# Attention on one Trainium2 core: the split maxima turned on their own and added by a product of three rows, the queries turned once

## What is computed

```python
q = (h @ w_q).reshape(b, l, N_HEADS, HEAD_DIM)        # 16 heads of 16
k = (h @ w_k).reshape(b, l, N_KV_HEADS, HEAD_DIM)     # 4 key heads
logits = jnp.einsum('bhqd,bkhd->bhqk', q, k) * scale
logits = jnp.where(causal[None, None], logits, -jnp.inf)
attn = jax.nn.softmax(logits, axis=-1)
ao = jnp.einsum('bhqk,bkhd->bqhd', attn, v).reshape(b, l, d)
```

## Time and profile before

| | |
|---|---|
| time, median of 3 runs | 2175.52 us (2172.95 to 2183.99) |
| the profiled execution | 2186.68 us, span 2185.4 us |
| busy: PE, PEld | 1665.2 us (76%), 1176.6 us (54%) |
| busy: DVE, ACT, POOL | 1023.0, 845.0, 457.5 us |

### The profile page before, as it was taken

One profiled execution on the slowest core, in us unless ns is written; L12 is line 12 of the kernel. 1 busy time (PEld: TensorE's weight loads), 2 busy tenths in 40 slices (PEclk: granted clock), 3 DMA queues, 4 the chain that ended last, 5 costly groups with the idle time before them and its releaser, 6 DMA issues. The chain is left out here.

```text
span 2185.4 us, 40696 instructions
## 1 busy us (share of the span) xinstructions
PE 1665.2 (76%) x16744; PEld 1176.6 (54%) x16744; DVE 1023.0 (47%) x1865; ACT 845.0 (39%) x1646; POOL 457.5 (21%) x511
## 2 busy tenths in 40 slices
PE   3678888888888888879888888783495577756958
PEld 2346665665666756657656666572253334433535
DVE  2435646556456566465565564633514543231131
ACT  2234444444444454444444444342221234411122
POOL 1111312322313222223132222231003201031100
PEclk9778999999989999899999899996698676767979
DMA  2101102111002011111110110101000000002010
GB/s 56 22 20 25 31 24 42 23 22 33 22 14 50 23 24 28 26 23 41 23 33 12 33 28 17 23 11 58 0 0 16 0 1 1 1 0 58 0 49 19
DMA packets 179800, 50.95 MB, mean 23 GB/s; under 512 B 151616, under 2 KB 174784, under 8 KB 179616
## 3 DMA queue, kind: packets, MB, share of 16 engines
q1 hardware_dynamic: 168240, 47.15, 9.7%
q10 hardware_dynamic: 11376, 1.19, 0.5%
HBM read 34.48 MB, written 13.83 MB: 22 GB/s over the span
## 5 line engine op out<-in xcount | busy, mean ns | idle before, releaser
L987 POOL TENSOR_TENSOR og<-og,sz 128x256 f32<-128x256 f32 x128 | 93.0, 726 | 753.4 <-DVE og L934 531.6
L435 PE MATMUL banks<-wv,xT 128*128 128x512 f32 x256 | 143.1, 711 | 74.3 <-DVE Yv L795 46.4
L795 DVE SCALAR_TENSOR_TENSOR Yv<-banks,cwall,Yv 128x1022 f32<-128x1022 f32 (+2 forms) x96 | 122.4, 1275 | 84.2 <-ACT Yv L651 83.6
L435 PE MATMUL banks<-wqk,xT 128*128 128x512 f32 x256 | 126.8, 641 | 23.8 <-DVE Yk L795 23.8
L435 PEld LDWEIGHTS banks<-wv,xT 128*128 128x128 f32 x256 | 55.3, 227 | 148.0 <-issue 148.0
L573 PE MATMUL banks<-wz,xT 128*128 128x256 f32 x512 | 132.0, 405 | 0.0
L638 PE MATMUL banks<-wo,oT 128*128 128x256 f32 x512 | 126.5, 391 | 0.8 <-ACT oT L788 0.8
L772 ACT ACTIVATE V<-banks,skd 128x128 f32<-128x128 f32 x192 | 59.9, 363 | 153.3 <-PE banks L602 153.0
L573 PEld LDWEIGHTS banks<-wz,xT 128*128 128x128 f32 x512 | 105.7, 209 | 23.1 <-issue 6.7
L638 PEld LDWEIGHTS banks<-wo,oT 128*128 128x128 f32 x512 | 95.6, 194 | 14.5 <-ACT oT L788 2.4
L617 PE MATMUL banks<-V,A 128*128 128x128 f32 x512 | 90.4, 305 | 11.9 <-ACT V L774 11.9
(11 more groups left out here) (332 smaller groups left out, 3758.0 us busy)
## 6 DMA issues: line engine op xcount, KB each, us to landing
cm_d<-CM SPq DMA_DIRECT2D x32, 256.0 KB, 4.2
wqk<-in_L_attn_W_qkvz SPq DMA_DIRECT2D x8, 512.0 KB, 4.5
wv<-in_L_attn_W_qkvz SPq DMA_DIRECT2D x8, 512.0 KB, 3.7
wz<-in_L_attn_W_qkvz SPq DMA_DIRECT2D x16, 256.0 KB, 2.8
wo<-in_L_attn_W_out SPq DMA_DIRECT2D x16, 256.0 KB, 3.0
blk<-cm_d SPq DMA_DIRECT2D x128, 16.0 KB, 1.8
t_d<-tb SPq DMA_DIRECT2D x16, 128.0 KB, 1.7
u_d<-ub SPq DMA_DIRECT2D x16, 128.0 KB, 1.8
```

Of the source, the lines that this page charges most:

```text
L435: ins = pe.matmul(bank[b][:, :], xT[:, d, b * S + of_batch, :], w[:, d, :], start=(d == 0), stop=(d == KD - 1))
L795: v.scalar_tensor_tensor(y, pair[0][:, :, 0:T - j], conv_w(k, t)[:, 3 - j:4 - j], y, ALU.mult, ALU.add).then_inc(s["tap"].sem, 1)
L987: pool.tensor_tensor(og[:, n, :, :], og[:, n, :, :], sz[q % 2][:, b, :].rearrange("p (h d) -> p h d", h=VR), ALU.mult).then_inc(s["osz"].s ...
```

## The change

The negated, split maxima no longer go into `qs`. They get a tile of their own, `n3`, with 32 columns for each `g` of which three are used. `pe_turn_max` turns it with 8 transposes for all four heads, and one ScalarE copy brings it to `nT`, where head `g` has rows 32`g` to 32`g`+2. The second turning of the queries, 32 transposes and four copies, is gone. In the scores by key the first product takes 96 rows in place of 128, and a new product of three rows, `one` by `nT`, of the same width, adds the maxima of each head. `n3` and `one` are filled once by GpSimd, ahead of its first copy of queries.

```diff
@@ -1400,26 +1400,37 @@
 
 
 def attention(nc, c, pair, bank, am, m, t_):
-    s = signals(nc, {"qs": 1, "qTt": 8, "qTe": 8, "sc": 16, "mx": 16, "nm": 6, "e": 16, "ex": 16, "pv": 8, "oTe": 2, "oTt": 2, "rec": 2, "on": 2})
+    s = signals(nc, {"qs": 1, "qTt": 4, "qTe": 4, "fill": 2, "nTt": 1, "nTe": 1, "sc": 16, "mx": 16, "nm": 6, "e": 16, "ex": 16, "pv": 8, "oTe": 2, "oTt": 2, "rec": 2, "on": 2})
     qb, qs, kT, vp, by_query, by_key = (t_[n] for n in ("qb", "qs", "kT", "vp", "by_query", "by_key"))
     qT = am("qT", [P, KVH, TT, P], BF16)
     mx, nm = am("mx", [P, TT, KVH]), am("nm", [P, TT, KVH])
+    n3, nT, one = am("n3", [P, TT, KVH, SLOT], BF16), am("nT", [P, TT, P], BF16), am("one_b", [P, P], BF16)
     pt, oT = am("ptile", [P, 2, KVH, T]), am("l1_oT", [P, T])
     rec, ao = am("rec", [P, QT, KVH]), am("ao", [P, TT, REP, KVH, HD])
     t_["ao"] = ao
 
     def on_gpsimd(pool):
+        pool.memset(n3[:, :, :, :], 0.0).then_inc(s["fill"].sem, 1)
+        pool.memset(one[:, :], 1.0).then_inc(s["fill"].sem, 1)
         for j in range(REP):
             if j:
-                pool.wait_ge(*s["qTt"](7, j - 1))
+                pool.wait_ge(*s["qTt"](3, j - 1))
             for i, part in enumerate(Q_PARTS):
                 ins = pool.tensor_copy(qs[:, :, :, i * HD:(i + 1) * HD], qb[:, part, :, j * KVH * HD:(j + 1) * KVH * HD].rearrange("p t (g e) -> p t g e", g=KVH))
             ins.then_inc(s["qs"].sem, 1)
 
-    def pe_turn_q(pe, j, go):
+    def pe_turn_max(pe, j):
+        pe.wait_ge(*s["qTe"](2, j))
+        for t in range(TT):
+            ins = pe.transpose(bank[4].bitcast(BF16)[:, t * P:(t + 1) * P], n3[:, t, :, :].rearrange("p g i -> p (g i)"), c["identb"][:, :])
+        ins.then_inc(s["nTt"].sem, 1)
+
+    def pe_turn_q(pe, j):
+        if j:
+            pe.wait_ge(*s["nTe"](0, j - 1))
         for g in range(KVH):
-            if g >= 2 or go:
-                pe.wait_ge(*s["qTe"](4 * go + g - 2, j))
+            if g >= 2:
+                pe.wait_ge(*s["qTe"](g - 2, j))
             for t in range(TT):
                 ins = pe.transpose(bank[4 + g % 2].bitcast(BF16)[:, t * P:(t + 1) * P], qs[:, t, g, :], c["identb"][:, :])
             ins.then_inc(s["qTt"].sem, 1)
@@ -1438,7 +1449,7 @@
         if b:
             pe.wait_ge(*s["on"](0, j))
         else:
-            pe.wait_ge(*s["qTe"](7, j))
+            pe.wait_ge(*s["qTe"](3, j))
         for u in range(QT):
             ins = pe.transpose(bank[5][:, u * P:(u + 1) * P], oT[:, u * P:(u + 1) * P], c["ident"][:, :])
         ins.then_inc(s["oTt"].sem, 1)
@@ -1448,7 +1459,7 @@
             if j:
                 pe.wait_ge(*s["on"](1, j - 1))
             pe.wait_ge(*s["qs"](0, j))
-            pe_turn_q(pe, j, 0)
+            pe_turn_q(pe, j)
             for t in range(TT):
                 b, q = divmod(t, QT)
                 width = (q + 1) * P
@@ -1464,18 +1475,21 @@
                         ins = pe.matmul(pair[gp][:, h, width - P:width], c["identb"][:, :], by_query[:, :], start=False, stop=True, skip_group_check=True)
                     ins.then_inc(s["sc"].sem, 1)
             pe.wait_ge(*s["nm"](5, j))
-            pe_turn_q(pe, j, 1)
+            pe_turn_max(pe, j)
             for b in range(B):
                 for kt in range(QT):
                     t = b * QT + kt
                     width = T - kt * P
                     for gp in range(2):
                         if t == 0:
-                            pe.wait_ge(*s["qTe"](4 + 2 * gp + 1, j))
+                            pe.wait_ge(*s["nTe"](0, j))
+                            pe.wait_ge(*s["fill"](1))
                         if t:
                             pe.wait_ge(*s["ex"](2 * (t - 1) + gp, j))
                         for h in range(2):
-                            pe.matmul(pair[gp][:, h, 0:width], kT[:, 2 * gp + h, t, :], qT[:, 2 * gp + h, t:(b + 1) * QT, :], start=True, stop=False, skip_group_check=True)
+                            pe.matmul(pair[gp][:, h, 0:width], kT[0:USED, 2 * gp + h, t, :], qT[0:USED, 2 * gp + h, t:(b + 1) * QT, :], start=True, stop=False, skip_group_check=True)
+                            rows = slice((2 * gp + h) * SLOT, (2 * gp + h) * SLOT + 3)
+                            pe.matmul(pair[gp][:, h, 0:width], one[rows, :], nT[rows, t:(b + 1) * QT, :], start=False, stop=False, skip_group_check=True)
                             ins = pe.matmul(pair[gp][:, h, 0:P], c["identb"][:, :], by_key[:, :], start=False, stop=True, skip_group_check=True)
                         ins.then_inc(s["e"].sem, 1)
                     if kt == 0 and j:
@@ -1495,14 +1509,13 @@
 
     def on_scalar(act):
         for j in range(REP):
-            for go in range(2):
-                for g in range(KVH):
-                    act.wait_ge(*s["qTt"](4 * go + g, j))
-                    if go:
-                        act.wait_ge(*s["sc"](15, j))
-                    elif j:
-                        act.wait_ge(*s["e"](15, j - 1))
-                    act.copy(qT[:, g, :, :], bank[4 + g % 2].bitcast(BF16).rearrange("p (t i) -> p t i", t=TT)).then_inc(s["qTe"].sem, 1)
+            for g in range(KVH):
+                act.wait_ge(*s["qTt"](g, j))
+                if j:
+                    act.wait_ge(*s["e"](15, j - 1))
+                act.copy(qT[:, g, :, :], bank[4 + g % 2].bitcast(BF16).rearrange("p (t i) -> p t i", t=TT)).then_inc(s["qTe"].sem, 1)
+            act.wait_ge(*s["nTt"](0, j))
+            act.copy(nT[:, :, :], bank[4].bitcast(BF16).rearrange("p (t i) -> p t i", t=TT)).then_inc(s["nTe"].sem, 1)
             for t in range(TT):
                 b, kt = divmod(t, QT)
                 width = T - kt * P
@@ -1525,12 +1538,15 @@
             v.wait_ge(*s["mx"](15, j))
             v.tensor_scalar(nm[:, :, :], mx[:, :, :], -1.0, None, ALU.mult).then_inc(s["nm"].sem, 1)
             v.wait_ge(*s["nm"](0, j))
-            v.wait_ge(*s["qTt"](3, j))
+            if j:
+                v.wait_ge(*s["nTt"](0, j - 1))
+            else:
+                v.wait_ge(*s["fill"](0))
             for i in range(3):
-                v.tensor_copy(qs[:, :, :, USED + i], nm[:, :, :]).then_inc(s["nm"].sem, 1)
+                v.tensor_copy(n3[:, :, :, i], nm[:, :, :]).then_inc(s["nm"].sem, 1)
                 v.wait_ge(*s["nm"](1 + 2 * i, j))
                 if i < 2:
-                    v.tensor_tensor(nm[:, :, :], nm[:, :, :], qs[:, :, :, USED + i], ALU.subtract).then_inc(s["nm"].sem, 1)
+                    v.tensor_tensor(nm[:, :, :], nm[:, :, :], n3[:, :, :, i], ALU.subtract).then_inc(s["nm"].sem, 1)
                     v.wait_ge(*s["nm"](2 + 2 * i, j))
             for b in range(B):
                 v.wait_ge(*s["oTt"](b, j))
```

## The result

The changed kernel takes 2267.38 us (median of 4 runs, 2264.86 to 2273.05), before it is 2174.25 us in the same measurement. The ratio is 1.0422, 95% interval 1.0385 to 1.0459: slower by 4.2%, where I had forecast 2.0% and a range that ended at 2244 us. The direction was right, and the size forecast was less than half of the one measured. The profiled executions have spans of 2185.4 and 2271.8 us, 86.4 apart.

The account below looks back on a forecast made before the run. TensorE was taken to bound the scores by key: 13.85 us added a round, less 1.24 of pauses and 1.79 for turning, gave +10.8, +43.3 in four; with +0.2 once, 2175.5 + 43.5 = 2219.0 us, range 2190 to 2244.

Parts of the forecast that it names:

- TensorE bounds the scores by key and gets all of the added work: In the scores by key, added TensorE work first fills 1.24 us of pauses, then lengthens the round.
- The turning, 1.79 us a round: Ahead of the scores by key: 8 transposes and one copy let the first product begin after 2.09 us, before 3.88.
- Once in the stage: GpSimd's fills of `n3` and `one` add 1.1 us, hiding the exponentials' table load saves about 0.9: together +0.2.
- The passage, 0.10 us: Scores by key: switching between whole-array and few-row products costs 0.10 us each way, 64 times a round, 6.4 us.
- The clock: In the scores by key, few-row products keep TensorE at 0.50 through tiles 0, 1 and the first values, then 1.00.
- the first values raise the clock: In the scores by key and values, the first values, with 128 rows and four heads side by side, bring 1.00.
- the pauses of 1.24: TensorE's waits in the scores by key that added work fills: 0.60, 0.24 and 0.40 us a round.
- 0.50 throughout: Rival: TensorE's clock stays at 0.50, columns of tiles 2 to 7 cost double, some 10 us a round more: 2259; chance 0.05.
- The early rise: Rival: the clock rises in tile 0 of the scores by key as before, 2.33 us a round less: 2209.7; chance 0.20.
- Cheap passages: Rival: switching to few-row products and back costs 0.05 us each way, 3.2 us a round less: 2206; chance 0.12.

Follow-up runs that it names:

- The kernel without the product: Against the changed kernel, the product adding the maxima is left out and the scores by key take 128 rows again: 2167.34 us, ratio 0.9948.
- The kernel with half the passages: Changed kernel reordered inside a pair of heads: both first products, then both three-row products, then both masks; 2238.38 us, ratio 1.0276.
- added pauses: Kernel with the maxima added over 128 rows, plus a three-row, 8-column product of zeros behind each of these products: 2223.74 us, ratio 1.0208.
- the version with copied maxima: Against the changed kernel, no second product: turned maxima are copied into rows 96 to 98 of `qT`, scores by key take 128 rows; 2172.53 us, ratio 0.9973.

## Why the prediction was right and wrong

**TensorE bounds the scores by key and gets all of the added work:** right. It is busy for 39.04 of 40.11 us there.

**The turning, 1.79 us a round:** right. From the first transpose (1826.65) to the first product (1828.79) are 2.14 us, forecast 2.09. The kernel without the product took 2167.34 us where these terms gave 2167; by its ratio it gained 11 us where they gave 7, so the exact hit has some luck in it.

**Once in the stage:** right in its parts. The fills took 0.95 and 0.21 us, forecast 0.88 and 0.2, and the table of exponentials was loaded by 1763.77, ahead of the first exponential at 1765.11, so all of it was hidden.

**The passage, 0.10 us:** right in sum. At 0.50, where 512 columns take 0.43: 0.57 from product to three-row product (1829.94 to 1830.51), 0.54 from there to the mask (to 1831.05), and 0.07 in place of 0.11 from the mask on. That is 0.14 + 0.11 - 0.04 = 0.21 a head and tile, where I had 0.20. The kernel with half the passages, where its expectation had 2252 for them alone, came out at 2238: its two three-row products took 0.54 us together, with which it would be 2235, and the clock was up for the end of one round.

**The clock: this is the step that failed.** The direction was right: behind products of fewer rows the clock came up later, 8.0 to 8.6 us behind the first product with 66 rows and 7.8 to 8.9 with 72, against 3.2 to 6.1 and 3.2 to 5.3 in their counterparts with 128. Its source, the scoring pass in the earlier trace rows, was read too simply, since the clock does not stay at 0.50 "through the pass": in the kernel before it is at 0.99 for the first 3.4 us of that pass (1743.50 to 1746.90), and it is up for a whole pass in the changed kernel's fourth round. What failed is that the first values raise the clock, from which followed "Tile 0, tile 1 and the first values then run at 0.50" and 1.00 for the rest. No row stood behind the part on the values: in the kernel before the clock was always up when they came. With 66 or 72 rows, and with added pauses, it did come up during the first values or up to 2.3 us behind them. In the changed kernel it stays at 0.50 for the whole of the stretch. What that costs can be had from the prediction's own terms, with every tile priced at 0.50. Per tile the four heads then cost 3.58 us more than before in tile 4, 2.92 in tiles 1 and 5, 2.29 in tiles 2 and 6, 1.65 in tiles 3 and 7, and 2.51 in tile 0; the values and the transposes of the leaving, which run at half speed too, about 4.7 in sum. That is 24.5 less the pauses of 1.24, 23.3 us; measured are 40.11 - 16.72 = 23.4. The forecast had 12.6. So all terms but the clock's were about right, and the clock's 10.8 us a round, 43 in four, are what was missed.

**The rival "0.50 throughout"** was named with 2259 us and a chance of 0.05. It is what happened. Its chance was too low: I had taken it as certain that the clock rises once many rows are at work, and asked only when. Its price left out that the next round's turning and first scores by query lose the clock as well: from the copy at 1868.90 to VectorE's first operation on the maxima of the next round it is 23.4 us (to 1892.27), and 22.2 at the same place in the kernel before (1870.41 to 1892.61), 1.2 more. Not every round pays it, since the fourth round's scores by query are at 1.00.

**The other rivals.** The early rise (2209.7) did not come. Cheap passages, 0.05 us, did not either: they took 0.14 and 0.11. The fourth head's three rows, 96 to 98, did not run beside its own 96-row product: the step is the same 0.54 us in every head (1832.87 to 1833.41 in the fourth). The runs show products of few rows side by side only where two three-row ones are neighbours, 0.54 us for both. And a busy TensorE, which was the argument for the early rise, did not bring the clock up: busy for 39.04 of 40.11 us, at 0.50 throughout.

**What stays open:** why the values do not raise the clock here, though with passages and no wide three-row columns it rose just behind them (11.0 to 12.1 us behind the first product), and why 96-row products run at 1.00 in some passes (1827.49 to 1839.92 in the version with copied maxima) and at 0.50 in others (1739.53 to 1754.79). The runs show both cases, not what decides between them.

## What to carry to other kernels

Removing work at the cost of a thin product was a bad trade here. The product of three rows took no less than one of 128 rows (512 columns at 0.50: 0.54 us with its passage against 0.43), going over to it and back cost 0.21 us, and the stretch of such products stayed at a clock of 0.50, at which 512 columns take 0.43 us in place of 0.22, for everything else in it too. Price such a change at both clock levels, and look for a row that shows the level behind just this mix; where the rows are free, pad the thin product to the full 128 (the change then cost 12 us in place of 92) or put the few rows into the spare rows of the product that is there anyway (6 us less than before).

## What the runs showed of the hardware

- With the same instructions and columns, TensorE's clock rose 8.0 to 8.6 us behind the first product with 66 rows and 3.2 to 6.1 us with 128 (four rounds each).
- With a three-row product behind each 96-row one, TensorE was busy for 97% of 40.11 us and the clock stayed at 0.50; with 128 rows for the three, it was at 1.00 after 4.4 us.
- Rows of zeros made a difference: 128 rows in place of 96 in the scores by query, the added ones zero, made the kernel 8 us faster, with the clock at 1.00 for all of three scoring passes in place of one.
- A three-row product of 512 columns took 0.54 us at 0.50 with its passage; two neighbouring ones, of two heads, took 0.54 together.
